# Folding the masked node groups before the scatter, gathering 3 and 4 tiles in turn, and reordering the setup of a four-layer graph kernel

## The chip, the cores and the metric

One core of one Trainium2 chip runs the whole program. The metric is device time in microseconds (us) of one launch. The chip's engines are named PE (TensorE, the matmul array), PEld (its weight loads), DVE (VectorE), ACT (ScalarE), POOL (GpSimd) and SP (SyncE, which only issues DMAs here).

## The reference, cut to what matters

Four message-passing layers on one graph of 3125 nodes and 100000 edges (`dst` is sorted, small node numbers being the most frequent; `src` is random), each followed by a residual and a layer norm over 16 features:

```python
edge_index = jnp.stack([src, dst])
x = _layernorm(x + L0(x, edge_index, edge_attr_16))               # mean of edge_attr_16 over dst
x = _layernorm(x + L1(x, edge_attr_48, edge_attr_3, ...))         # two equivariant convolutions, scattered by src
x = _layernorm(x + L2(x, edge_attr_2, edge_index, ...))           # edge network, gathers x[src], scatters by dst
x = _layernorm(x + L3(x, edge_index, W1, b1, W2, b2))             # two GCN layers
```

The last one, on which most of the change falls:

```python
def gcn_conv(h, W, b):
    hw = h @ W
    msg = hw[row] * norm[:, None]                       # row = src and the self loops
    return segment_sum(msg, col, num_segments=N) + b    # col = dst and the self loops
h = jnp.tanh(gcn_conv(x, W1, b1))
h = jnp.tanh(gcn_conv(h, W2, b2))
```

## The kernel before

Edges are padded to 98 groups (`NSUP`) of 1024; a group has T = 8 tiles of 128 edges, one edge to a partition. Nodes are padded to 25 blocks (`NB`) of 128. Since `dst` is sorted, a group touches only a few neighbouring blocks; DVE computes a table of windows (first block, last block, running offset) at the start, and every scatter by `dst` loops over the blocks of a group's window. A "window" below is one group with one block of its window. Passes run one after the other:

- **Setup** (lines 893 to 977): constants, the window tables, then from L945 on three blocks that only later passes need: the split of `src` into a fifth (`src_h`) and a rest (`src_v`, `src_n`), the same for `src` as rows on 98 partitions (`row_f`, `row_h`, `row_v`, stored by SP to the DRAM table `vtab`), and the unit edge vectors `rhat` (L969 to L977, with a square root on ACT).
- **Mean** (PE L665 to L684, DVE L994 to L1006): pairs of groups. SP's `load_pair` (L312) loads `edge_attr_16`, ACT and POOL split it into three bf16 parts (`high_part`, `rest_of`, `mid_part`, `low_part`; four pairs ahead), DVE makes one-hots of `dst`, PE scatters. Four pair buffers stand between them.
- **L1's two convolutions** (`for l in range(2)`), PE, ACT and DVE all busy. DVE's first product waits for POOL's gather from the table that SP stored (`s_tab`).
- **Edge pass** (p = 2), pairs of groups, gathering and scattering.
- **GCN passes** (p = 3, 4). POOL gathers the rows of the first GP = 3 tiles of a group by indirect DMA into `gr`, a ring of R = 4 groups. The other PT = 5 tiles are gathered by PE: DVE compares a broadcast row of `vtab` with the partition number (L1334, 5 instructions, `oht`), PE multiplies that one-hot with the table in SBUF (L824, 5 matmuls of 240 columns for a tile, into three PSUM banks of 2, 2 and 1 tiles), and DVE masks the result with the one-hot of the fifth (L1346, `mk`, 240 columns for a tile: 5 candidate fifths of 48, of which only one is not zero). PE then scatters by `dst`: a POOL-gathered tile takes one matmul of 48 columns (L836), a PE-gathered tile three of 80 columns (L840), 18 matmuls for a window. The one-hots of `dst` for it are made by ACT, window by window: 8 ACTIVATEs (L585) and one over all 8 tiles (L590), into a ring of R = 4 windows (`of_used` frees them). PE's program order is: gather of group s+1, scatter of group s. DVE's is: `tile_onehots(s+2)`, `select_rows(s+1)`. SP, per group: wait for POOL's gather of s, load the indices of s+4, wait for `oht` of s, load the `vtab` row of s+2. The end of a pass reduces 5 PSUM banks (L1405), adds, applies tanh, multiplies by the weights and builds the next table.

Of the kernel before, what the change touches and what calls it, by code (L numbers as in the profile page):

```python
# [38 lines left out]
GP = 3  # L39
PT = T - GP  # L40
# [7 lines left out]
ABANK = 512 // AW  # L48
# [14 lines left out]
def build(nc, a):  # L63
    with ExitStack() as ctx:
# [11 lines left out]
        mk = sb("mk", [P, 2, T, GW], BF16)  # L76
        mkf = mk[:, :, :, :].rearrange("p b t n -> p b (t n)").bitcast(F32)[:, :, 0:T * AW]\
# [82 lines left out]
        row_f = ht[0:NSUP, 0, :]  # L160
        row_h = ht[0:NSUP, 1, :]
# [61 lines left out]
        of_used = {p: sem(f"of_used{p}") for p in (3, 4)}  # L223
        row_used = [sem(f"row_used{p}") for p in range(2)]
# [62 lines left out]
        def _(sp):  # L287
# [20 lines left out]
            sp.wait_ge(s_rowv, 1)  # L308
            sp.dma_start(vtab, row_v).then_inc(s_vtab, 16)

            def load_pair(i, r):  # L312
                sp.wait_ge(ea_lo, i * R + r + 1)
                for b in range(2):
                    sp.dma_start(ea16[:, r, b, :, :].rearrange("p t f -> p (t f)"),
                                 e16[bass.ds(i * 2 * R + 2 * r + b, 1), :, :].rearrange("o p f -> p (o f)")).then_inc(ea_in[r], 16)

            with sp.Fori(0, PAIRS // R) as i:
                for r in range(R):
                    load_pair(i, r)  # L320
            load_pair(PAIRS // R, 0)
# [12 lines left out]
            for p in range(2):  # L334
# [8 lines left out]
                store_table(p)  # L343
                with sp.Fori(1, PAIRS) as i:
# [29 lines left out]
            def load_tail(p, b, s):  # L374
                sp.dma_start(vb[:, b, 0:PT * P], vtab[bass.ds(s, 1), GP * P:SUP].broadcast_to([P, PT * P]))\
                    .then_inc(vb_in[p][b], 16)

            for p in (3, 4):
# [3 lines left out]
                for r in range(R):  # L382
                    if p == 3 and r < 2:
                        sp.wait_ge(g_in[2][r], (QUADS + 1 - r) * 16 * T)
                    elif p == 4:
                        sp.wait_ge(g_in[3][r], (ROUNDS + (1 if r < 2 else 0)) * 16 * GP)
# [3 lines left out]
                def refill_ring(i, r, more):  # L390
                    s = i * R + r
                    if more:
                        sp.wait_ge(g_in[p][r], (i + 1) * 16 * GP)
# [17 lines left out]
        def _(pool):  # L411
# [25 lines left out]
            def gather(p, b, seen):  # L437
# [3 lines left out]
                for t in range(T if p == 2 else GP):  # L441
# [47 lines left out]
        def _(act):  # L489
# [13 lines left out]
            root(rn_root, rn[:, :, :].rearrange("p s t -> p (s t)"))  # L503
# [8 lines left out]

            high_part(0, 0, 1)
            with act.Fori(0, PAIRS // R) as i:
                for r in range(R):
                    high_part(i * R + (r + 1), (r + 1) % R, i + (1 if r + 1 < R else 2))
                    mid_part(i * R + r, r)
            mid_part(PAIRS - 1, 0)
            act.wait_ge(s_par, 16 * 21)
            node_root()  # L520
            node_root()
            for l in range(2):
# [51 lines left out]
            for p in (3, 4):  # L574
                def window_onehots(i, r):
                    s = i * R + r
                    lo, hi, off = load_window(act, s)
                    with act.Fori(lo, hi) as c:  # L578
# [4 lines left out]
                        for t in range(T):  # L583
# [3 lines left out]
                        act.wait_ge(of_abs[p], (off + c) * T + T)  # L587
                        act.sem_inc(s_turn, 1)
                        oh = oh_f[:, bass.ds(turn, 1), :, :].rearrange("p o t n -> p (o t n)")
                        nc.scalar.activation(oh, oh, ACT.Relu, bias=ones[:, 0:1], scale=-1.0).then_inc(of_ready[p], 1)  # L590

                act.sem_inc(of_abs[p], BIAS * T)
# [13 lines left out]
        def _(pe):  # L606
# [53 lines left out]
            pe.wait_ge(s_par, 16 * 21)  # L660

            for bk in range(4):
                zero_bank(bk)
            def mean_step(j, r):  # L665
# [20 lines left out]

            for l in range(2):
# [117 lines left out]
            for p in (3, 4):  # L805
                for bk in range(5):
# [5 lines left out]
                def sums_of(c):  # L812

                    at = pe.snap(c * AW + ((c * 43) >> 8) * (512 - ABANK * AW), min_val=0, max_val=5 * 512 - AW)
                    return at

                def gather_tiles(s, b):

                    pe.wait_ge(oht_done[p], s * NC + NC)
                    for g in range(3):  # L820
                        pe.wait_ge(mk_done[p], s * 3 + (g + 1))
                        for t in range(2 * g, min(2 * g + 2, PT)):
# [4 lines left out]
                        mm.then_inc(gm_done[p], 1)  # L827
# [668 lines left out]
```

## Time and profile before

| | |
|---|---|
| median of 3 runs | 4139.42 us (4136.7 to 4139.91) |
| profiled execution | 4135.05 us, of it 4133.2 us span |
| busy share of the span | PE 84%, DVE 79%, ACT 71%, POOL 65% |
| mean | about 71.5 to 246 us |
| L1, first and second convolution | 270 to 1350, 1393 to 2421 us |
| edge pass | 2445 to 3062 us |
| GCN passes 3 and 4 | 3110 to 3604, 3625 to 4118 us |
| mean granted TensorE clock | 0.93 |

Times in the profile count from the first instruction. The time of a run is about 2 us more than the span. The boundaries of the passes were read off the timeline.

### The profile page before, as it was taken

To read this page: it belongs to the slowest core of one execution; us is meant where nothing else is said; L and a number is where in the kernel's file an instruction comes from. 1 tells how busy PE (TensorE), PEld (TensorE's weight loads), DVE (VectorE), ACT (ScalarE), POOL (GpSimd) and SP (SyncE) were. 2 spreads that over 40 slices of the span, in tenths; PEclk is the share of its full clock that TensorE was granted. 3 is DMA by queue.
4 is the path that set the end of the run, shared out by engine and by line. 5 is a ranking of instruction groups with operands and counts; after the bars stand their busy time and mean duration, and the time that the engine had idled before them with its cause. 6 is when DMAs were issued, how large, how long until landed. Compare 5 with 4: busy or idle time off the path is not lost.

```text
span 4133.2 us, 104667 instructions
## 1 busy us (share of the span) xinstructions
PE 3490.8 (84%) x29279; PEld 2953.1 (71%) x29280; DVE 3285.2 (79%) x6447; ACT 2937.3 (71%) x4368; POOL 2696.7 (65%) x2653
## 2 busy tenths in 40 slices
PE   1569999999999699999999967778868988789886
PEld 1448888888888477777777757777757777678775
DVE  7769999999999688888888878888877765577655
ACT  1239999999999599999999930000017888888887
POOL 2547777777776577777777747776626655366553
PEclk9999999999999799999999988777769998899988
DMA  5112111111111311111111111111103222122221
GB/s 62 37 21 25 24 25 24 24 25 24 25 24 23 23 30 30 30 29 30 31 30 31 30 21 31 29 29 26 26 8 49 47 39 37 26 49 46 39 38 24
DMA packets 282518, 126.21 MB, mean 31 GB/s; under 512 B 178158, under 2 KB 257202, under 8 KB 282486
## 3 DMA queue, kind: packets, MB, share of 16 engines
q1 hardware_dynamic: 200950, 97.56, 10.1%
q0 software_dynamic: 81536, 28.26, 8.0%
q8 instruction: 16, 0.26, 0.0%
q14 instruction: 16, 0.13, 0.0%
HBM read 123.81 MB, written 1.78 MB: 30 GB/s over the span
## 4 chain that ended last, share of the span: by engine, by line
PE 26%; issue 21%; POOL 17%; DVE 13%; ACT 11%; ACTq 6%; DVEq 3%; DMA 2%; SPq 1%; POOLq 0%
POOL gb L452 16%; PE ps L706 10%; PE ps L722 10%; ACT rest L585 9%; ACTq L585 2%; ACTq L280 2%; PE ps L712 2%; PE ps L619 2%; DVE oht L1266 2%; DVE oh L989 2%; DVE rest L1005 1%; ACTq L578 1%; PE ps L824 1%; DVE xt L1091 1%; ACT v L571 1%
## 5 line engine op out<-in xcount | busy, mean ns | idle before, releaser
L452 POOL DMA_INDIRECT gb<-table,idx x1568 | 1617.2, 1031 | 555.0 <-issue 450.1
L442 POOL DMA_INDIRECT gb<-table,idx x980 | 984.6, 1005 | 710.3 <-issue 432.2
L706 PE MATMUL ps<-big,oh 128*128 128x290 f32 (+1 forms) x7840 | 1264.0, 308 | 1.7 <-DVE big L1131 1.7
L706 PEld LDWEIGHTS ps<-big,oh 128*128 128x128 f32 x7840 | 1069.7, 191 | 124.5 <-DVE big L1131 2.2
L722 PE MATMUL ps<-w,ht 128*128 128x320 f32 x3136 | 1007.7, 444 | 103.7 <-DVE xt L1091 102.1
L532 ACT ACTIVATE oh<-iota_f,src_n 128x640 fp32r<-128x640 f32 x1372 | 1024.5, 815 | 0.0
L535 ACT ACTIVATE oh<-oh,ones 128x2560 fp32r<-128x2560 f32 (+1 forms) x392 | 849.6, 2167 | 12.8
L722 PEld LDWEIGHTS ps<-w,ht 128*128 128x128 f32 x3136 | 556.9, 191 | 365.3 <-DVE xt L1091 173.6
L1091 DVE TENSOR_TENSOR xt<-ps,gb 128x640 f32<-128x640 f32 x784 | 643.8, 821 | 91.1 <-PE ps L722 27.2
L585 ACT ACTIVATE rest<-rest,dst_f x1952 | 595.9, 387 | 116.7 <-issue 96.1
L824 PE MATMUL ps<-tabb,oht 128*128 128x240 bf16 x4900 | 593.9, 283 | 35.6 <-DVE oht L1334 13.4
L1099 DVE TENSOR_REDUCE msg<-xt 128x80 f32<-128x1280 f32 (+1 forms) x392 | 580.7, 1482 | 0.0
L824 PEld LDWEIGHTS ps<-tabb,oht 128*128 128x128 bf16 x4900 | 495.0, 104 | 100.6 <-issue 31.4
L1346 DVE TENSOR_TENSOR mk<-ps,oh_h 128x480 bf16<-128x480 f32 (+1 forms) x588 | 316.5, 570 | 277.1 <-PE ps L824 272.8
L571 ACT ACTIVATE v<-v 128x384 fp32r<-128x384 f32 x98 | 51.3, 523 | 561.0 <-DVE v L1281 437.2
L1131 DVE TENSOR_TENSOR big<-parts,oh_h 128x1160 fp32r<-128x1160 f32 (+1 forms) x392 | 426.9, 1089 | 0.2
L775 PE MATMUL ps<-tabb,oht 128*128 128x80 bf16 x5880 | 293.6, 229 | 73.7 <-DVE mk L1295 60.7
L775 PEld LDWEIGHTS ps<-tabb,oht 128*128 128x128 bf16 x5880 | 287.1, 118 | 79.4 <-DVE mk L1295 65.5
L1334 DVE TENSOR_SCALAR oht<-eat,pid_c 128x640 bf16<-128x640 f16 x980 | 322.2, 394 | 24.8 <-DMA eat<-vtab 24.6
L590 ACT ACTIVATE rest<-rest,ones x244 | 280.1, 1148 | 30.0
L619 PE MATMUL ps<-v,oh 128*128 128x96 f32 x1168 | 178.9, 316 | 79.1 <-DVE oh L989 72.7
L525 ACT ACTIVATE ht<-ps,b 113x512 f32<-113x512 f32 x196 | 134.6, 687 | 151.4 <-PE ps L712 151.4
(225 smaller groups left out, 2672.6 us busy)
## 6 DMA issues: line engine op xcount, KB each, us to landing
gb<-table,idx POOLq DMA_INDIRECT x2548, 2.4
eat<-in_eat SPq DMA_DIRECT2D x196, 192.0 KB, 2.4
eat<-vtab SPq DMA_DIRECT2D x196, 160.0 KB
eat<-vtab SPq DMA_DIRECT2D x49, 256.0 KB
rest<-in_edge_attr SPq DMA_DIRECT2D x98, 64.0 KB, 1.8
idx<-in_src SPq DMA_DIRECT2D x245, 4.0 KB
idx<-in_dst SPq DMA_DIRECT2D x196, 4.0 KB, 1.6
ea<-in_edge_attr SPq DMA_DIRECT2D x1, 784.0 KB, 19.5
```

Source lines behind the costliest of these rows:

```text
L442: nc.gpsimd.indirect_dma_start(out=(gb if p == 2 else gr)[:, b, t, 0:tabw[p]], out_offset=None, in_=tabs[p], in_offset=bass.IndirectOffset ...
L452: nc.gpsimd.indirect_dma_start(out=gb[:, b, t, 0:tabw[p]], out_offset=None, in_=tabs[p], in_offset=bass.IndirectOffsetOnAxis(ap=idx[:, b, ...
L532: nc.scalar.activation(oh5[:, b, t, :], iota_f[:, 0:CW], ACT.Abs, bias=src_n[:, bass.ds(s, 1), t]).then_inc(a_abs[l], 1)
L535: nc.scalar.activation(oh5[:, b, t0:t1, :], oh5[:, b, t0:t1, :].bitcast(F32), ACT.Relu, bias=ones[:, 0:1], scale=-1.0).then_inc(a_done[l], 1)
L585: nc.scalar.activation(oh, iota_h[:, bass.ds(c * P, P)], ACT.Abs, bias=dst_f[:, bass.ds(s, 1), t], scale=-1.0).then_inc(of_abs[p], 1)
L706: mm = nc.tensor.matmul(out, oh5[:, b, t, c * P:(c + 1) * P], big[:, b, t, 0:W], start=False, stop=False, skip_group_check=True)
L722: mm = nc.tensor.matmul(ps[:, WPAIR[l][t // 2 % 2] + c, 0:MJ * D], ht[:, b, (t // 2) * P:(t // 2 + 1) * P], w2[l][:, c, :], start=True, st ...
L775: mm = nc.tensor.matmul(ps[:, 5 + g, u * AW:(u + 1) * AW], oht[:, k, c, e:e + P], tabk[:, c, part, :, :], start=(c + part == 0), stop=(c = ...
L824: mm = nc.tensor.matmul(ps[:, 5 + g, (t % 2) * GW:(t % 2 + 1) * GW], oht[:, b, c, t * P:(t + 1) * P], tabc[:, c, :, :], start=(c == 0), st ...
L1091: V.tensor_tensor(pv, wv, repeat(xin, 2, J_), ALU.mult).then_inc(p_done[l], 1)
L1099: V.tensor_reduce(msg[:, b, 4 * h:4 * h + 4, 0:J_], pv, AX.X, ALU.add).then_inc(r_done[l], 1)
L1131: V.tensor_tensor(big[:, b, 4 * h:4 * h + 4, 0:NH * MP[l]].rearrange("p t (h f) -> p t h f", h=NH), repeat(parts[l][:, b, 4 * h:4 * h + 4, ...
```

## The change

1. **Fold (`compact_rows`, new).** After the masks, DVE adds the five candidate fifths of every PE-gathered tile together in three bf16 adds: 96 columns to 96, 48 to 48, and the last 48 into `mc`. Only one fifth is not zero. PE scatters the folded row with one matmul of 48 columns, so a window takes 8 matmuls in place of 18. The sums fill 3 PSUM banks in place of 5, zeroed and reduced accordingly.
2. **3 and 4 tiles in turn.** Even groups keep 3 POOL-gathered tiles, odd groups get 4 (`GPS`); PE gathers 5 or 4 (`TAIL`), the latter in two PSUM banks.
3. **Setup.** The `src` split and `rhat` move on DVE from ahead of the mean to behind the table of L1's first convolution; the row split moves behind the table of the second one, and SP's store of `vtab` with it. `load_pair` moves from SP's queue to ACT's, four pairs ahead by hand. PE's wait for the parameters moves behind the mean. ACT's root of `rn` comes third, not first.

```diff
@@ PE: scatter, GCN
                 def scatter_tiles(at, ohs, r):
                     for t in range(T):
-                        if t < GP:
-                            mm = nc.tensor.matmul(psf[:, bass.ds(at, 3 * D)], ohs(t), gr[:, r, t, 0:3 * D // 2].bitcast(BF16),
-                                                  start=False, stop=False, skip_group_check=True)
-                        else:
-                            for n in range(3):
-                                mm = nc.tensor.matmul(psf[:, bass.ds(at, AW)], ohs(t), mk[:, r % 2, t - GP, n * AW:(n + 1) * AW],
-                                                      start=False, stop=False, skip_group_check=True)
+                        rows = gr[:, r, t, 0:3 * D // 2].bitcast(BF16) if t < GPS[r % 2] else mc[:, r % 2, t - GPS[r % 2], :]
+                        mm = nc.tensor.matmul(psf[:, bass.ds(at, 3 * D)], ohs(t), rows,
+                                              start=False, stop=False, skip_group_check=True)
...
-                    pe.wait_ge(mk_done[p], s * 3 + 6)
+                    pe.wait_ge(mc_done[p], s + 1)
@@ POOL
-                for t in range(T if p == 2 else GP):
+                for t in range(T if p == 2 else GPS[b % 2]):
@@ DVE: GCN
+                def compact_rows(s, b):
+                    m = TAIL[b]
+                    dve.wait_ge(mk_done[p], s * 3 + 6)
+                    V.tensor_tensor(mk[:, b, 0:m, 0:6 * D], mk[:, b, 0:m, 0:6 * D], mk[:, b, 0:m, 6 * D:12 * D],
+                                    ALU.add).then_inc(ad_done[p], 1)
+                    dve.wait_ge(ad_done[p], s * 2 + 1)
+                    V.tensor_tensor(mk[:, b, 0:m, 0:3 * D], mk[:, b, 0:m, 0:3 * D], mk[:, b, 0:m, 3 * D:6 * D],
+                                    ALU.add).then_inc(ad_done[p], 1)
+                    dve.wait_ge(ad_done[p], s * 2 + 2)
+                    V.tensor_tensor(mc[:, b, 0:m, :], mk[:, b, 0:m, 0:3 * D], mk[:, b, 0:m, 12 * D:15 * D],
+                                    ALU.add).then_inc(mc_done[p], 1)
                 def step(i, r, more):
...
                         select_rows(s + 1, 1 - r % 2)
+                        compact_rows(s + 1, 1 - r % 2)
@@ ACT: loads of the mean
+            for r in range(R - 1):
+                load_pair(0, r)
             high_part(0, 0, 1)
-            with act.Fori(0, PAIRS // R) as i:
+            with act.Fori(0, PAIRS // R - 1) as i:
                 for r in range(R):
                     high_part(i * R + (r + 1), (r + 1) % R, i + (1 if r + 1 < R else 2))
                     mid_part(i * R + r, r)
+                    if r == 0:
+                        load_pair(i, R - 1)
+                    else:
+                        load_pair(i + 1, r - 1)
```

Not shown: the DVE lines that move whole (L945 to L953 and L964 to L977 to behind L1073; L955 to L962 to behind L1211), the constants, and the semaphore counts that follow from them.

## Rows read from the trace of the kernel before

**Rows 1.** Busy time by stretch; columns PE, PEld, DVE, ACT, POOL, clock, DMA.
```profile
core 0: us, PE busy (x) PEld busy (x) DVE busy (x) ACT busy (x) POOL busy (x), PEclk, DMA share, GB/s
...
71.50:246.40 174.90, 93.80 (x1218) 82.18 (x1218) 128.90 (x220) 34.32 (x91) 86.30 (x91) 1.00 0.12 34
...
270.50:1350.00 1079.50, 1056.50 (x5678) 864.83 (x5678) 991.27 (x1568) 979.39 (x974) 825.21 (x779) 1.00 0.14 24
...
3110.00:3604.00 494.00, 421.09 (x4695) 363.87 (x4695) 324.98 (x868) 422.73 (x1063) 277.04 (x290) 0.92 0.23 41
```

**Rows 2.** Waits in pass 3: who for whom, us, times, longest.
```profile
DVE mk L1346 <- PE ps L824: 137.6, 124, 5.0
...
PE ps L836 <- ACT rest L590: 46.7, 23, 2.5
...
ACT rest L585 <- PE ps L840: 10.9, 3, 5.3
```

**Rows 3.** Timeline of ACT in pass 3, window starts; 12 windows left out.
```profile
3121.48 2.45 ACT L585 ACTIVATE rest<-rest,dst_f  x8 [5.29 <-PE ps L840]
...
3180.64 2.44 ACT L585 ACTIVATE rest<-rest,dst_f  x8 [0.48 <-issue]
3184.26 2.43 ACT L585 ACTIVATE rest<-rest,dst_f  x8
```

**Rows 4.** Timeline of one group in pass 3.
```profile
3133.44 2.73 PE L824 MATMUL ps<-tabb,oht 128*128 128x240 bf16 x25
3133.48 0.19 DVE L1328 TENSOR_TENSOR oh_h<-src_h,iota_f 128x25 f32<-128x25 f32 x1 [0.16 <-DVE mk L1346]
3133.65 1.68 DVE L1334 TENSOR_SCALAR oht<-eat,pid_c 128x640 bf16<-128x640 f16 x5
...
3134.90 0.95 POOL L442 DMA_INDIRECT gb<-table,idx  x1 [0.30 <-issue]
3135.26 1.52 DVE L1346 TENSOR_TENSOR mk<-ps,oh_h 128x480 bf16<-128x480 f32 x3
...
3136.94 0.19 DVE L1328 TENSOR_TENSOR oh_h<-src_h,iota_f 128x25 f32<-128x25 f32 x1 [0.16 <-DVE mk L1346]
```

**Rows 5.** Timeline of pass 3's last groups and end.
```profile
3587.13 4.40 PE L824 MATMUL ps<-tabb,oht 128*128 128x240 bf16 x25
...
3602.01 1.18 PE L840 MATMUL ps<-mk,rest 128*128 128x80 bf16 x15
...
3603.30 3.01 DVE L1405 TENSOR_REDUCE t<-ps 128x96 f32<-128x480 f32 x5 [7.95 <-PE ps L830]
```

**Rows 6.** Timeline of DVE in the setup.
```profile
22.45 0.53 DVE L946 CAST src_f<-src_i 128x784 f32<-128x784 int32 x1
...
37.80 0.69 DVE L956 CAST ht<-acc 98x1024 f32<-98x1024 int32 x1 [9.57 <-DMA acc<-in_src_row]
...
66.98 2.61 DVE L977 TENSOR_TENSOR rhat<-rhat,rn 128x2352 f32<-128x2352 f32 x1
...
71.55 0.23 DVE L1000 TENSOR_SCALAR rest<-dst_f,rest 128x16 f16 x1 [1.96 <-issue]
```

**Rows 7.** Timeline of DVE where L1's two convolutions begin.
```profile
257.38 0.57 DVE L1072 COPY tab<-x 128x400 f32<-128x400 f32 x1
...
270.50 0.82 DVE L1091 TENSOR_TENSOR xt<-ps,gb 128x640 f32<-128x640 f32 x1 [12.55 <-DMA gb<-table,idx]
...
1392.74 0.26 DVE L1141 TENSOR_TENSOR vprod<-gb,rhat 128x96 f32<-128x96 f32 x1 [22.43 <-DMA gb<-table,idx]
```

**Rows 8.** Groups of POOL: edge pass (first row), pass 3 (second).
```profile
L442 POOL DMA_INDIRECT gb<-table,idx x392 | 422.2, 1077 | 203.5 <-issue 151.3 <-DVE v L1281 51.3 <-DMA idx<-in_src 0.9
...
L442 POOL DMA_INDIRECT gb<-table,idx x290 | 277.4, 956 | 197.6 <-PE ps L830 111.7 <-issue 85.9
```

**Rows 9.** Groups of DVE by form: a mask of two tiles.
```profile
L1346 DVE TENSOR_TENSOR mk<-ps,oh_h 128x480 bf16<-128x480 f32 x392 | 253.9, 655 | 275.5 <-PE ps L824 271.4 <-issue 1.5
```

**Rows 10.** DVE's line 1005, duration ns min/median/max.
```profile
L1005 DVE TENSOR_TENSOR rest<-rest x146: 678/692/1165, 71.8 to 244.8; 128x1024 bf16<-128x1024 f16 x146
```

More of the change, by code:

```diff
@@ L38 @@
 EH = 64
-GP = 3
-PT = T - GP
+GPS = (3, 4)
+GP = min(GPS)
+OA = T
+TAIL = [T - n for n in GPS]
+GROUPS = [[2, 2, n - 4] for n in TAIL]
 MID = NP_ // 2
@@ L223, in build @@
         of_used = {p: sem(f"of_used{p}") for p in (3, 4)}
+        ad_done = {p: sem(f"ad_done{p}") for p in (3, 4)}
+        mc_done = {p: sem(f"mc_done{p}") for p in (3, 4)}
         row_used = [sem(f"row_used{p}") for p in range(2)]
@@ L343, in _ @@
                 store_table(p)
+                if p == 1:
+                    sp.wait_ge(s_rowv, 1)
+                    sp.dma_start(vtab, row_v).then_inc(s_vtab, 16)
                 with sp.Fori(1, PAIRS) as i:
@@ L501, in stat_root, with load_pair @@
                 root(sv_root[:, :], sv[:, 0:D])
-            root(rn_root, rn[:, :, :].rearrange("p s t -> p (s t)"))
+            def load_pair(i, r):
+                act.wait_ge(ea_lo, i * R + r + 1)
+                act.sem_inc(s_turn, 1)
+                for b in range(2):
+                    nc.scalar.dma_start(ea16[:, r, b, :, :].rearrange("p t f -> p (t f)"),
+                                        e16[bass.ds(i * 2 * R + 2 * r + b, 1), :, :].rearrange("o p f -> p (o f)")).then_inc(ea_in[r], 16)
             def high_part(j, r, seen):
@@ L517, in _ @@
                     mid_part(i * R + r, r)
+                    if r == 0:
+                        load_pair(i, R - 1)
+                    else:
+                        load_pair(i + 1, r - 1)
+            for r in range(R):
+                high_part(PAIRS - R + r, (r + 1) % R, PAIRS // R + (r + 1) // R)
+                mid_part(PAIRS - R - 1 + r, r)
+                if r == 0:
+                    load_pair(PAIRS // R - 1, R - 1)
+                elif r == 1:
+                    load_pair(PAIRS // R, 0)
             mid_part(PAIRS - 1, 0)
-            act.wait_ge(s_par, 16 * 21)
             node_root()
             node_root()
+            root(rn_root, rn[:, :, :].rearrange("p s t -> p (s t)"))
+            act.wait_ge(s_par, 16 * 21)
             for l in range(2):
@@ L582, in window_onehots @@
                         act.sem_inc(s_turn, 1)
-                        for t in range(T):
+                        for t in range(OA):
                             oh = oh_f[:, bass.ds(turn, 1), t, :].rearrange("p o n -> p (o n)")
@@ L805, in _ @@
             for p in (3, 4):
-                for bk in range(5):
+                for bk in range(-(-NB // ABANK)):
                     zero_bank(bk)
@@ L1211, in _ @@
                     dve.sem_inc(s_node, 1)
+                    dve.wait_ge(s_row, 16)
+                    link(V.tensor_copy(row_f, row_i))
+                    link(V.tensor_scalar(row_h, row_f, float(CW), None, ALU.is_ge))
+                    for k in range(2, NH):
+                        link(V.scalar_tensor_tensor(out=row_h, in0=row_f, scalar=float(k * CW), in1=row_h,
+                                                    op0=ALU.is_ge, op1=ALU.add))
+                    V.scalar_tensor_tensor(out=row_v, in0=row_h, scalar=-float(CW), in1=row_f,
+                                           op0=ALU.mult, op1=ALU.add).then_inc(s_rowv, 1)
                 else:
```

113 lines of the change are left out of this document (51 added, 62 removed).

## Prediction

> **What bounds the kernel now.** I first cut the span into its passes with the table of stretches [rows 1] and asked of each which engine has no room. The change touches three places.
>
> In the setup and the mean nothing is full: DVE is busy 128.90 of 174.90 us of the mean, and it works alone on the path before it. The timeline shows when the mean may begin: the window tables are ready at 22.45 us, but the first one-hot starts at 71.55 us, behind blocks that the mean doesn't read, one of them preceded by an idle wait of 9.57 us for a DMA [rows 6]. L1's first convolution is PE's (1056.50 of 1079.50 us), so a shift of its start moves everything behind it by as much.
>
> In passes 3 and 4 PE is busy 421.09 of 494.00 us and ACT 422.73 [rows 1], which alone names no bound. The waits do: ACT's L585 waited for PE's scatter only 3 times, 10.9 us in all, while PE waited for ACT's L590 23 times and DVE for PE 124 times [rows 2]. The rest of ACT's idle time is its own issue. ACT's windows start every 4.23 us (59.16 us for the 14 windows from 3121.48 to 3180.64), and 3.62 us apart where a second window of the same group follows, at 3184.26, for the first time in group 19 [rows 3]. So the pass goes at ACT's pace, 122 windows of about 4.05 us, and ACT's work is what the change leaves alone. The scatter's matmuls, which the change cuts from 18 to 8, are not on that path.
>
> **Setup.** DVE's work from 22.45 to 69.6 us (end of L977 [rows 6]) leaves the head of the mean: the first one-hot comes 71.55 − 24.5 = 47.0 us earlier, if the 1.96 us of loop entry stay. It can come so early only if pair 0 is loaded and split. SP used to issue these loads at 45 us, behind everything; ACT can now issue from about 15 us, when POOL's reduction has passed. Loading then takes place beside the big strided loads. I take 1.5 us for that, so −45.5 us. Bounds: 0 lost, and 13.3 lost if the new loads queue behind SP's until `src_row` has landed at 37.8 [rows 6]: 37.8 minus 24.5.
>
> ACT's six to eight extra DMA issues per four pairs cost nothing: ACT is busy 34.32 of 174.90 us in the mean [rows 1], and the four buffers of a ring hide its latency. If they didn't, each of 49 pairs would lose up to the length of two issues, under 1 us.
>
> What comes back: behind `tab` (end 257.95) DVE idled 12.55 us until the gathered rows were there [rows 7]. Now the `src` split takes 5.8 us (22.45 to the end of L953 at 28.2), the constants 2.1, and the `rhat` block 22.8 (46.8 to 69.6, its wait for ACT's root included): 30.7 us. The first product comes 30.7 − 12.5 = 18.2 us later. POOL's gathers, PE's weights and ACT's one-hots are then ready earlier than needed, but each of them has small buffers, so nothing is won by it. The row split (37.80 to 44.25, 6.4 us) goes under the 22.43 us in which DVE waits before 1392.74 [rows 7]; the store of `vtab` behind it delays SP's later loads by as much, and they are due 10 us a group. Cost nothing; without that cover 6.4 us. The 9.57 us of waiting vanish. Sum of the setup: −45.5 + 18.2 = −27.3 us (from −28.8 to −15.5).
>
> **Passes 3 and 4, what is removed.** At the end of a pass, behind ACT's last window, 15 + 3 matmuls become 8: 1.18 us of L840 [rows 5] become some 0.5, so −0.65. L1405's five reductions of 3.01 us [rows 5] become two of 480 elements and one of 240, some 1.7: −1.3. Early in the pass window 5 is released by a scatter (5.29 us of ACT's waiting [rows 3]), which is 10 matmuls shorter: −0.4. Together −2.4 us a pass. Zeroing 3 banks, not 5, is hidden under DVE's building of the table.
>
> **What is added.** DVE's round for a group takes 3.46 us when nothing keeps it waiting (3133.48 to 3136.94 [rows 4]). The three adds stand nowhere in this trace. Nearest from below are 16-bit operands in SBUF: 1024 elements in 0.692 us [rows 10], 25 elements in 0.19 [rows 4], so 0.49 ns an element beyond 0.18: 480, 240 and 240 elements take 0.42 + 0.30 + 0.30 and 0.03 us for each wait on its own result, 1.1 us. Nearest from above is the mask, 480 elements in 655 ns [rows 9]: 0.66 + 0.42 + 0.42 + 0.09 = 1.6 us. I take 1.1, since both operands are 16-bit there as here. An odd group has a fifth less of `oht` (−0.32), 240 fewer masked elements (−0.24) and adds of four fifths the size (1.0). So DVE needs 4.6 and 3.9 us in turn, 4.25 on average (4.7 with the upper price), against ACT's 4.23 in groups of one window.
>
> POOL: gathers start 1.25 us apart (0.95 and 0.30 idle [rows 4]), 3.75 us a group. Now 3.5 a group: 4.38 us. And they get company: in the edge pass, where DVE runs many instructions with both inputs in SBUF, the same gather takes 1077 ns, not 956 [rows 8], which makes 3.5 × 1.377 = 4.82 us. I take 1.30 a gather, 4.55 us: DVE's new adds are short and fill about a fifth of its round. The Trainium skill (SBUF — State Buffer, "Who interferes with whom") says that a VectorE instruction with two SBUF inputs contends with a GpSimd instruction that reads SBUF, and that the later one blocks until the other is done. The masks of before have one input in PSUM, the adds two in SBUF, so by this rule the adds speak against this change; by row alone (4.38) a pass would lose 2.7 us, by the edge pass's number 10.6 (below).
>
> So POOL at 4.55 and DVE at 4.25 are both slower than ACT's 4.23, but only where groups have one window. That is so for groups 1 to 18. From there on two-window groups give 24 windows for 20 groups up to group 39, then more, about 4.9 us a group, and ACT is the bound again. What ACT falls behind in the first stretch it never regains: (4.55 − 4.23) × 18 = 5.8 us, less a little that the ring has in hand, 5.5. Bounds: (4.38 − 4.23) × 18 = 2.7, or 0 if the ring takes it, and (4.82 − 4.23) × 18 = 10.6.
>
> The PE queue loses 10 matmuls a window and 2.5 a group; PE was waiting for ACT anyway. Nobody waits longer behind DVE's adds: PE reads the folded row only after the gather of the next group, 2.73 us at full clock [rows 4].
>
> A pass: −2.4 + 5.5 = +3.1, both +6.2.
>
> **Sum.** −27.3 + 6.2 = −21.1 us. From the profiled 4135.05 us that gives 4114.0; the median of the runs is 4.4 us higher, so 4118.3, say 4118.
>
> **Rivals.**
> *Passes 3 and 4 stay ACT's in full.* For: DVE idles 137.6 us a pass, POOL's average is under ACT's 5.04 a group. Against: both averages hide the first stretch. −28 − 4.8 gives 4106.
> *POOL is blocked as in the edge pass.* For: the rule above and 1077 ns. Against: the adds are shorter than the edge pass's 1.2 us one-hots. 10.6 to 12 a pass: −27.3 − 4.8 + 24 = −8, 4131.
> *The new loads come late.* For: in 15 to 33 us SP's loads fill the DMA engines. Against: separate queues. The mean begins 13.3 us later: 4118 + 12 = 4130. The Trainium skill (DMA: Bandwidth & Descriptors, "Issuing engines are not separate DMA queues") says that DMAs started by different engines run on the same 16 engines and interleave; by this the loads would be neither free nor last in line.
> *TensorE's clock falls, on the other side.* PE has less to do, and its clock in pass 3 was already 0.92 of full [rows 1]; where it waited for ACT it fell to 1.2 GHz and 25 gather matmuls took 4.40 us, not 2.73 [rows 4, 5]. At that level a one-window group costs 22.5 matmuls × 0.176 = 4.0, the scatter 0.7 and about 0.6 of gaps, 5.3 us against ACT's 4.23. Over the first 39 groups, 43 windows and 171 us, that is up to 34 us a pass: −27.3 − 4.8 + 68 = +36, 4175. It decides where more than half of those groups run at the low clock. Against: at 5.3 us PE would have no pauses, and in the stretches where it had none the clock was up.
>
> **Chances.** Forecast 0.50 (its own range 4110 to 4126), ACT's pace kept 0.17, POOL blocked 0.12, late loads 0.13, clock 0.05, something else 0.03. A measurement here tells 0.2%, 8.3 us, from no change, so below 4131.1 is faster. The first two are, with half of the next two: 0.78. The other halves are "same", with part of the rest: 0.16. Slower 0.06. The range: 4105 to 4135 takes in the kept pace, blocked POOL and late loads, and leaves out the clock and the case in which two of the bad ones meet.
>
> **What would show it.** The first L1000 at 24 to 27 us; the last matmul of the mean near 200; the first L1091 near 243; from there to pass 3 everything 27 us earlier and otherwise alike. In passes 3 and 4: three adds of 0.42, 0.30 and 0.30 us; L442 between 0.97 and 1.02 us; ACT waiting for PE's scatter in the first 20 groups, some 0.3 us a window on average, and hardly after; passes of 495 to 500 us. Wrong would be: L1000 after 35 us; ACT waiting in the second half of a pass; a mean clock under 0.8 there; adds over 0.5 us.

## The result, and the profile after

| | before | changed |
|---|---|---|
| median of 18 runs, us | 4137.81 (4134.86 to 4142.38) | 4130.03 (4124.27 to 4134.66) |
| ratio, 95% interval | 1 | 0.9981 (0.9973 to 0.9988) |
| span of the profiled execution, us | 4133.2 | 4131.1 |

The change gained 7.8 us, 0.19%; from the same median the forecast of 4118 us is a gain of 19.8. The measured 4130.03 us lies inside the stated range of 4105 to 4135, but the gain is less than half of the 21.1 us that the sum gave. One thing must be known to read the experiments: they were timed in five sets, each with runs of the kernel before beside them, and that kernel took 4,141 us in the second set and 5,101 to 5,104 us in the other four, so ratios are compared within a set alone. Of stretches, the mean can be compared across sets: from its first window to its last, five kernels with the setup of before took 172.33 to 172.43 us, in whichever set they ran.

The spans of the two profiled executions differ by 2.1 us, the medians by 7.8. A term that is read from one trace late in the kernel is therefore good to some 6 us only; the mean's terms are much better than that.

The table of stretches, changed kernel: the mean, L1's first convolution, pass 3 (columns as in [rows 1]).

```profile
24.70:216.70 192.00, 94.39 (x1221) 82.12 (x1219) 136.44 (x220) 38.55 (x100) 86.73 (x98) 1.00 0.23 46
259.20:1340.50 1081.30, 1057.87 (x5679) 865.71 (x5679) 991.28 (x1570) 979.28 (x974) 815.81 (x768) 0.99 0.14 24
3101.00:3599.00 498.00, 404.61 (x3235) 321.19 (x3235) 383.50 (x1108) 422.95 (x1063) 321.86 (x339) 0.85 0.24 38
```

The timeline of DVE, changed kernel: the mean's first one-hot, the first step behind the mean, the first product of L1 and of its second convolution, the sums at the end of pass 3.

```profile
24.75 0.23 DVE L979 TENSOR_SCALAR rest<-dst_f,rest 128x16 f16 x1 [2.22 <-issue]
...
216.64 0.18 DVE L1040 TENSOR_SCALAR r<-ps 128x25 f32<-128x25 f32 x1 [0.86 <-PE ps L698]
...
259.26 0.82 DVE L1096 TENSOR_TENSOR xt<-ps,gb 128x640 f32<-128x640 f32 x1
...
1382.77 0.26 DVE L1146 TENSOR_TENSOR vprod<-gb,rhat 128x96 f32<-128x96 f32 x1 [15.86 <-DMA gb<-table,idx]
...
3599.06 1.79 DVE L1436 TENSOR_REDUCE t<-ps 128x160 f32<-128x480 f32 x3 [7.53 <-PE ps L847]
```

Against [rows 6, 7, 5] the first one-hot is 46.8 us earlier (line 979 prepares it, so its start is taken as the mean's). L1's first product is only 11.2 us earlier, its second convolution 10.0, the end of pass 3 4.2, the end of the span 2.1. The mean, 174.90 us before [rows 1], takes 192.00. The loss is there.

Where in the mean? DVE's line 979 (1000 before) runs once for each of the 73 windows. From the first start to the last it is 172.40 us before (71.55 to 243.95) and 189.46 after (24.75 to 214.21). The first 8 of these 72 spacings take 19.52 and 24.84 us, the other 64 take 152.88 and 164.62. So 17.06 us are two losses: 5.32 at the start and 11.74 spread over all the rest. The timeline at the start, changed kernel:

```profile
23.65 1.28 ACT L509 ACT_TABLE_LOAD   x1 [23.49 <-PEq L674]
...
24.95 0.72 ACT L509 ACTIVATE rest<-rest 128x256 bf16<-128x256 f32 x2
...
25.45 1.85 POOL L418 TENSOR_TENSOR rest<-rest 128x256 f32<-128x256 f32 x2 [10.61 <-ACT rest L509]
...
28.48 1.17 PE L688 MATMUL ps<-rest 128*128 128x49 bf16 x16 [2.85 <-POOL rest L423]
...
29.28 1.68 DVE L984 TENSOR_TENSOR rest<-rest 128x1024 bf16<-128x1024 f16 x2 [1.32 <-PE ps L688]
...
32.45 0.42 ACT L509 ACTIVATE rest<-rest 128x256 bf16<-128x256 f32 x1 [3.67 <-DMA rest<-in_edge_attr]
```

ACT may split the first pair only when PE has released its buffer (L674), which PE does behind its wait for the setup. DVE begins the one-hots of pair 0 at 25.02 us, but the product waits for the split until 28.48, 3.73 us after line 979 first starts. Before, four pairs had been split long ahead, and the same distance was 1.10 us (71.55 to 72.65). The last line shows the second part of the price: ACT then waits 3.67 us for a load of a later pair.

The groups of DVE over the last 65 windows, kernel before (first fence) and changed kernel (second): first the one-hots themselves (two for a window), then the step ahead of them. Idle time stands behind the second bar.

```profile
L1005 DVE TENSOR_TENSOR rest<-rest 128x1024 bf16<-128x1024 f16 x128 | 97.9, 806 | 4.2 <-PE ps L674 2.0
L1000 DVE TENSOR_SCALAR rest<-dst_f,rest 128x16 f16 x65 | 15.8, 243 | 36.1 <-DVE rest L1005 32.8 <-issue 3.3
```

```profile
L984 DVE TENSOR_TENSOR rest<-rest 128x1024 bf16<-128x1024 f16 x128 | 103.1, 846 | 3.8 <-PE ps L688 1.7
L979 DVE TENSOR_SCALAR rest<-dst_f,rest 128x16 f16 x65 | 16.2, 249 | 42.2 <-issue 23.5 <-DVE rest L984 18.7
```

The loss has two halves at the same code. The idle time ahead of the window's first step rose by 6.1 us (36.1 to 42.2), and the label changed with it: "issue", time that nothing in the profile releases, went from 3.3 us to 23.5. The one-hots got slower by 5.2 us (97.9 to 103.1). One of them takes 0.69 us, or some 0.47 us more; of the 130 of these windows 35 were long before and 45 are now. The changed kernel's timeline has both kinds:

```profile
65.25 1.29 DVE L984 TENSOR_TENSOR rest<-rest 128x1024 bf16<-128x1024 f16 x2
...
66.00 1.08 POOL L418 TENSOR_TENSOR rest<-rest 128x256 f32<-128x256 f32 x1 [0.85 <-ACT rest L509]
...
67.66 0.23 DVE L979 TENSOR_SCALAR rest<-dst_f,rest 128x16 f16 x1 [1.11 <-issue]
...
67.88 0.66 POOL L418 TENSOR_TENSOR rest<-rest 128x256 f32<-128x256 f32 x1 [0.17 <-ACT rest L509]
67.93 2.23 DVE L984 TENSOR_TENSOR rest<-rest 128x1024 bf16<-128x1024 f16 x2
...
68.50 1.12 POOL L423 TENSOR_TENSOR rest<-rest 128x256 bf16<-128x256 f32 x1
```

Two one-hots take 1.29 us, and 2.23 us where POOL's subtractions run beside both. Such windows are 2 of 65 before, with 1.7 us of POOL's work beside them, and 12 of 65 now, again with 1.7. So a later turn also moves DVE's one-hots onto POOL's subtractions. That this overlap is what lengthens them is read from the timelines; no run took it away by itself.

A pair with one window mostly takes 2.43 or 2.37 us before and 2.67 after. The 64 spacings hold 40 turns of the outer loop, which took 101.5 us before and 110.25 after, 0.22 us more each. The 24 second windows of a pair, which the inner loop brings, took 51.4 and 54.4 us; 12 of them before and 11 now come after the shortest time, 1.89 or 1.90 us. So it is the turn of the outer loop that got slower, and the longer one-hots add to it.

### The profile page after: what moved, and what is told of

Read it like the earlier page. It is cut to its first block, busy times and chain, and to the rows that moved or that the text cites. A ratio compares the mean times of both kernels' runs of the same rounds, so it can differ in the third digit from the quotient of the medians.

```text
span 4131.1 us, 99865 instructions
## 1 busy us (share of the span) xinstructions
PE 3454.0 (84%) x26345; PEld 2866.4 (69%) x26346; DVE 3410.5 (83%) x6933; ACT 2938.7 (71%) x4369; POOL 2786.3 (67%) x2751
## 4 chain that ended last, share of the span: by engine, by line
PE 25%; issue 22%; POOL 18%; DVE 14%; ACT 10%; ACTq 6%; DVEq 4%; DMA 2%; POOLq 0%; SPq 0%
POOL gb L448 16%; PE ps L721 10%; PE ps L737 10%; ACT rest L601 8%; ACTq L601 2%; PE ps L727 2%; DVE oht L1280 2%; ACTq L286 2%; DVE oh L968 1%; POOL gb L438 1%; PE ps L635 1%; DVE rest L984 1%; ACTq L594 1%; DVE xt L1096 1%; ACT v L587 1%
## 5 line engine op out<-in xcount | busy, mean ns | idle before, releaser
L448 POOL DMA_INDIRECT gb<-table,idx x1568 | 1620.5, 1033 | 571.4 <-issue 451.4
L438 POOL DMA_INDIRECT gb<-table,idx x1078 | 1075.1, 997 | 630.2 <-issue 452.6
L841 PEld LDWEIGHTS ps<-tabb,oht 128*128 128x128 bf16 x4410 | 469.6, 110 | 121.3 <-DVE mk L1363 31.5
L1363 DVE TENSOR_TENSOR mk<-ps,oh_h 128x480 bf16<-128x480 f32 (+1 forms) x490 | 273.9, 596 | 160.4 <-PE ps L841 159.9
L790 PEld LDWEIGHTS ps<-tabb,oht 128*128 128x128 bf16 x5880 | 294.1, 120 | 84.5 <-DVE mk L1309 70.6
L1349 DVE TENSOR_SCALAR oht<-eat,pid_c 128x640 bf16<-128x640 f16 (+1 forms) x980 | 313.2, 385 | 30.8 <-DMA eat<-vtab 29.3
```

Source lines behind the costliest of these rows:

```text
L438: nc.gpsimd.indirect_dma_start(out=(gb if p == 2 else gr)[:, b, t, 0:tabw[p]], out_offset=None, in_=tabs[p], in_offset=bass.IndirectOffset ...
L448: nc.gpsimd.indirect_dma_start(out=gb[:, b, t, 0:tabw[p]], out_offset=None, in_=tabs[p], in_offset=bass.IndirectOffsetOnAxis(ap=idx[:, b, ...
L790: mm = nc.tensor.matmul(ps[:, 5 + g, u * AW:(u + 1) * AW], oht[:, k, c, e:e + P], tabk[:, c, part, :, :], start=(c + part == 0), stop=(c = ...
L841: mm = nc.tensor.matmul(ps[:, 5 + g, (t % 2) * GW:(t % 2 + 1) * GW], oht[:, b, c, t * P:(t + 1) * P], tabc[:, c, :, :], start=(c == 0), st ...
```

## Experiments

**Which part costs what.** The setup part alone, and the convolution part alone, each on the kernel before (the hunks of the diff, nothing new).

> The setup part alone (row splits, unit directions and constants behind the mean, the loads of edge_attr_16 issued by ACT), with the graph convolutions of before. Theory 1 (the two parts are independent, and each has the price seen in the trace of the changed kernel): the first product of L1 stands at 259 us in place of 270.5, the mean needs 192 us from its first to its last window in place of 175, passes 3 and 4 keep their lengths, and the time is 9 to 11 us under before (ratio 0.9974 +- 0.0004). Rival (part of the loss in passes 3 and 4 came from the setup's shift, through the throttle of TensorE's clock): passes 3 and 4 are longer here as well, by 2 us or more together, and the time is only 5 to 8 us under before.

> The convolution part alone (fold of the masked groups, one scatter matmul for each tile, POOL 3 and 4 tiles in turn), with the setup of before. Theory 1: the mean and L1 stand where they stand before (first product of L1 at 270.5 us), and passes 3 and 4 together cost 6.8 us more, so the time is 4144 to 4146 us (ratio 1.0016 +- 0.0004). Rival (the loss in the passes is an interaction with the setup part): the ratio is 1.0005 or less.

Both were timed in the first set, with the kernel before at 5,104 us. The setup part gave 0.9939 (0.9913 to 0.9964); its 72 spacings took 188.09 us (24.76 to 212.85), so the mean's loss belongs to the setup part. The convolution part gave 1.0248 (1.0218 to 1.0278), far from either expectation. It was run again:

> The same kernel as b_conv: the convolution part alone. Theory: passes 3 and 4 cost 6.8 us together and nothing else moves, so the ratio to before is 1.0016 +- 0.0005. Rival (they cost this only together with the setup part): 1.0005 or less.

In the second set: 1.0011 (1.0002 to 1.0020), 3.5 us slower by the medians, with 6.8 just inside the interval's 0.8 to 8.3 us. The parts are independent as far as this can tell. What the other sets show is taken up at the end.

**The mean: is it the loads?** First the loads of `edge_attr_16` back on SP, ACT's loop as before; then SP's other loads held back.

> The changed kernel with the loads of edge_attr_16 issued by SP again, behind its 25 setup loads; everything else as changed. Theory T1 (the loads in ACT's queue are what makes each pair of the mean slower): one pair with one window takes 2.43 us again, and from its first to its last window the mean needs about 175 us plus what its start costs. Theory T2 (where DVE's loop lies among its instructions, once the setup steps ahead of it are gone, makes each turn of the outer loop some 0.2 us longer): a pair still takes 2.67 us, and the drift of 12 us over 49 pairs stays. Either way the first pairs wait longer for their rows, since they are issued behind SP's other loads: the first window at 30 to 45 us in place of 24.75. By T1 the mean ends near 210 to 220 us, by T2 near 222 to 235 us.

> The changed kernel with all of SP's loads behind dst held until eight pairs of the mean have been split (one wait on POOL's low parts): src, edge_attr_3, edge_attr_2, x, the row form of src and the parameters, none of which is used before the mean ends at 217 us. Theory (the first 5.3 us that the mean lost by window 8 came from its rows landing beside these big loads): the gap to the spacing of before by window 8 falls from 5.3 us to 1 us or less, the later drift of 0.24 us per pair stays unless it too is made by the loads, and the mean ends at 211 to 214 us; time 3 to 5 us under the changed kernel. Rival (the early loss is ACT's issue time or the order of the steps, not the big loads): the mean ends at 216 to 218 us as in the changed kernel, and the time is equal to it. If T1 holds, holding the loads has no effect on the later drift.

```diff
             sp.dma_start(dst_i[:, :, :], dstv).then_inc(s_dst, 16)
+            sp.wait_ge(ea_lo, R + 8)
             sp.dma_start(src_i[:, :, :], srcv).then_inc(s_src, 16)
```

With SP's loads the last 64 spacings took 165.28 us, so T1 falls: who issues the loads has nothing to do with the drift. (The first window came at 24.82 us all the same, not at 30 to 45, and the mean ended at 236.9.) What ACT's issuing does buy is the start; with SP DVE waited 23.40 us for the second pair, behind SP's own loads:

```profile
51.02 2.18 DVE L976 TENSOR_TENSOR rest<-rest 128x1024 bf16<-128x1024 f16 x2 [23.40 <-PE ps L680]
```

With the other loads held back the first 8 spacings took 23.43 us in place of 24.84, the rest 163.37. So the loads beside SP's big ones cost 1.4 us, near the 1.5 that the prediction took for it, and not the 5.3 that this experiment's theory gave it; 3.9 us of the early loss stay. The 1.4 is a difference of two traces from different sets, and the first 8 spacings of kernels with this code range from 24.84 to 25.39 us.

**The mean: is it the loop's place?** Semaphore increments that nobody waits for, ahead of the window tables, move the loop along DVE's stream. Places are counted in the built program: the outer loop's 21 instructions begin at the 65th in the changed kernel and at the 92nd before.

```diff
+            for _ in range(27):
+                dve.sem_inc(s_idle, 1)
             dve.wait_ge(s_extp, 1)
```

> The changed kernel with 27 semaphore increments, which nothing waits for, put into DVE's stream ahead of the window tables, so that the mean's loop stands at the place among DVE's instructions (the 92nd to the 112th) that it had before; nothing else is changed. Theory T2 (the place of the loop makes each turn 0.24 us longer): a pair with one window takes 2.43 us again, the last window starts 12 us sooner after the first than in the changed kernel (about 177 us in place of 189.5), the mean ends at 204 to 206 us, and the time is 10 to 12 us under the changed kernel's. Rival (the turns are longer for something that the streams of the other engines, or the data in flight, bring): a pair takes 2.67 us, and the mean ends at 216 to 218 us.

> The changed kernel with one semaphore increment ahead of DVE's window tables: the mean's loop begins at DVE's 66th instruction in place of the 65th, counted in the built program. If what counts is the place by a small step (the loop's head at a multiple of 2, 4 or more), a pair with one window takes 2.43 us at once; if it is how far from the start of the stream the loop lies, or a boundary that the longer shift of 27 crossed, it stays 2.67 us.

> The changed kernel with one more semaphore allocated and nothing that uses it, so the semaphores named behind it have other numbers and no instruction moves. If the one extra instruction of k_pad1 was what ended the drift (the loop's place), a pair with one window takes 2.67 us here as in the changed kernel; if it was the semaphores' numbers, 2.43 us.

> The kernel before with five semaphore increments ahead of DVE's window tables: the mean's loop begins at DVE's 97th instruction, 32 behind its place in the changed kernel, so with the same remainder by 4, 8, 16 and 32. If the remainder counts, a pair with one window takes 2.67 us in place of 2.43, and the mean is 11 to 12 us longer with nothing else changed; if the distance from the start counts, it stays 2.43 us.

> The kernel before with 37 semaphore increments ahead of DVE's window tables: the mean's loop begins at DVE's 129th instruction of the built program, 64 behind its place in the changed kernel (the 65th). If the loop is slow where its head comes at a multiple of 64 instructions, a pair with one window takes 2.67 us and the mean 11 to 12 us more, in a kernel whose work is otherwise that of before; if it stays at 2.43 us, a period of 64 is out as well, and what the place means stays open.

> The changed kernel with three short steps (the identity, the node numbers and the mask of real nodes) moved from ahead of the mean behind it, so that the mean's loop begins at DVE's 62nd instruction of the built program in place of the 65th, and all its setup stays otherwise as changed. If there is a boundary in the stream between the 65th and the 66th instruction, with the loop's head ahead of it and its body behind, a turn of the outer loop still crosses it here, and a pair with one window takes 2.67 us; if only that one place of the head is slow, 2.43 us, and the time is 11 us under the changed kernel's.

> The changed kernel with 256 semaphore increments ahead of DVE's window tables: the loop begins at DVE's 321st instruction, 256 behind its place in the changed kernel. 
| kernel | loop begins at | last 64 spacings, us |
|---|---|---|
| before | 92nd | 152.88 |
| before + 5 | 97th | 152.83 |
| before + 37 | 129th | 152.93 |
| changed | 65th | 164.62 |
| changed, one semaphore more, no instruction | 65th | 164.35 |
| changed + 1 | 66th | 153.55 |
| changed + 27 | 92nd | 154.02 |
| changed, three steps moved away | 62nd | 162.11 |
| changed + 256 | 321st | 163.00 |

Each row is one trace; other kernels with the head at the 65th and nothing added (setup part, 3 gathers, 4 gathers, no adds) give 163.0 to 164.9 us, so the two levels lie some 10 us apart with a spread of 2.

The group of line 979's counterpart in the changed kernel + 27 (with its one-hots), + 1 and + 256, one fence for each:

```profile
L987 DVE TENSOR_TENSOR rest<-rest 128x1024 bf16<-128x1024 f16 x128 | 98.5, 810 | 4.2 <-PE ps L689 2.2
L982 DVE TENSOR_SCALAR rest<-dst_f,rest 128x16 f16 x65 | 15.7, 241 | 36.3 <-DVE rest L987 31.9 <-issue 4.4
```

```profile
L982 DVE TENSOR_SCALAR rest<-dst_f,rest 128x16 f16 x65 | 15.8, 243 | 35.8 <-DVE rest L987 31.5 <-issue 4.3
```

```profile
L982 DVE TENSOR_SCALAR rest<-dst_f,rest 128x16 f16 x65 | 16.2, 249 | 42.8 <-issue 22.5 <-DVE rest L987 20.2
```

One instruction more takes "issue" from 23.5 us to 4.3, and the idle time from 42.2 to 35.8; with 27 more the one-hots are back at 98.5 us, 36 of 130 long. So both halves of the loss hang on the loop's place. With the head at the 66th, all of the loop lies behind the place between the 65th and the 66th; with the head at the 65th or 62nd the loop crosses it twice in a turn. The idle time that this adds is 6.1 us over 40 turns, 0.15 us a turn; with what it does to the one-hots a turn takes 0.22 us more. With the head 256 instructions further on the same happens; at 92, 97 and 129 it doesn't. The first boundary is pinned to one place, between the 65th and the 66th. The second lies somewhere in the loop's 21 instructions from the 321st on, so 256 to 275 behind the first. The fast places exclude one each 32 or each 64 (the 97th and the 129th lie 32 and 64 behind the 65th); one each 128 was not tried. (The 256 increments took 22.4 us, the first window coming at 47.14, more than the 5 to 16 expected.)

The changed kernel + 27 was timed in the second set and gave 0.9938 (0.9923 to 0.9953), 4116.32 us: the change as written with its loop elsewhere is 24.3 us faster than before. The mean gives 10.9 us of what it has over the changed kernel. Between L1's first product (248.33) and the first product of the second convolution (1367.04; 259.26 and 1382.77 in the changed kernel) another 4.8 us come, which were not expected. The increments move every later loop of DVE too. By the built programs the loop of L1's first convolution, 77 instructions and 48 turns, begins at the 172nd in the changed kernel, at the 179th before and at the 199th with the 27. The traces of the second set and of the result fall apart the same way:

| kernel | L1's loop begins at | first product to that of the second convolution, us |
|---|---|---|
| before | 179th | 1122.24 |
| convolution part alone | 179th | 1123.62 |
| changed | 172nd | 1123.51 |
| changed, 3 gathers | 172nd | 1125.77 |
| changed + 27 | 199th | 1118.71 |
| faults of the mean mended (below, also with the 27) | 199th | 1117.21 |

DVE's idle time put down to "issue" ahead of line 1096 falls from 24.9 to 20.2 us with the 27. A boundary 128 behind the first, between the 193rd and the 194th, would do this, some 0.1 us a turn; one each 256 would not touch this loop in any of the six. No mean loop of the first table lies across the 193rd. So 128 fits both tables, but no run moved L1's loop by itself, and the distance stays open.

**What the passes pay.** The fold kept with 3 gathers in each group; the fold's adds left out; 4 gathers in each group.

```diff
-GPS = (3, 4)
+GPS = (3, 3)
```

> The changed kernel with POOL gathering 3 tiles of every group, as before, and the fold kept, so DVE masks 5 tiles of every group. Theory (POOL's 3.5 gathers a group are what lost 0.2 us in each of the 18 groups with one window): ACT sets these groups' pace again, the 3.7 us that each pass lost by its 24th window go, and the time is 5 to 8 us under the changed kernel's. Rival (DVE, with the masks and adds of a group, is as late as POOL): the groups take 4.5 us or more, each pass loses 1 to 3 us more than in the changed kernel, and the time is 2 to 6 us over the changed kernel's.

> The changed kernel with the three adds of the fold left out: the scatter reads the first 48 of the 240 masked columns (so four of the five node groups are left out of the masked tiles' rows), in one matmul for a tile as before. Theory (DVE's masks and adds, 4.3 us a group where POOL's gathers and TensorE's products allow it, set the pace of the 18 groups with one window): DVE has 0.9 us a group less to do, ACT sets the pace again, the first 24 windows of a pass take 107 to 110.5 us in place of 114.3 and 111.2, and the time is 5 to 8 us under the changed kernel's. Rival (POOL's four gathers in every second group): the first 24 windows keep 111 to 114 us, and the time is within 2 us of the changed kernel's.

> The changed kernel with POOL gathering 4 tiles of every group, so DVE masks and adds 4. Theory (DVE sets the pace): DVE has 0.5 us a group less than with 3.5 gathered tiles' average, but POOL then needs 4 gathers of 0.95 us and the gaps between them, near 4.3 to 5 us a group; if POOL becomes the bound, the first 24 windows of a pass take 114 to 120 us, and the time is 2 to 15 us over the changed kernel's. Rival (POOL can keep 4 gathers a group inside 4.3 us): ACT sets the pace and the time is 3 to 6 us under the changed kernel's.

The windows of a pass are marked by the start of ACT's Relu. Pass 4 first. From the 9th to the 17th there is one window a group: 33.68 us before (4.21 a group), 34.55 in the changed kernel (4.32), 34.61 in the convolution part alone (4.33), 34.92 with 3 gathers (4.37). In pass 3 the same eight groups take 33.88, 35.02, 34.18 and 34.21 us, and in the changed kernel + 27, the same code, 33.98 and 34.22 in the two passes. So the eight groups tell before (4.21 to 4.24 a group) from the fold (4.25 to 4.38), but not the variants of the fold from each other. The table of stretches for these eight groups in pass 4, changed kernel, then 3 gathers and fold:

```profile
3649.27:3683.82 34.55, 29.12 (x239) 23.42 (x239) 30.96 (x91) 28.75 (x72) 26.27 (x28) 0.92 0.26 45
```

```profile
3651.62:3686.54 34.92, 31.93 (x276) 25.84 (x273) 33.60 (x97) 28.88 (x72) 24.90 (x25) 1.00 0.26 48
```

And POOL's group in the same stretch of the changed kernel:

```profile
L438 POOL DMA_INDIRECT gb<-table,idx x28 | 26.6, 951 | 8.5 <-issue 8.5
```

In the changed kernel POOL waits for nothing but its own issue: 26.6 + 8.5 us fill the 34.55, so POOL has no room. With 3 gathers POOL has room and DVE is busy 33.60 of 34.92 us, so DVE is the likely bound. The first 24 windows take 112.1 and 110.4 us in passes 3 and 4, against 110.3 and 107.1 before and 114.3 and 111.2 changed: part of the loss comes back, not all, and both theories are half right. The time was 0.9972 (0.9962 to 0.9982) of before, 4129.32 us, not to be told from the changed kernel's.

The other two were timed in two of the other sets, with the kernel before at 5,104 and at 5,101 us:

> The same kernel as i_noadds (the fold's adds left out). From the trace of the changed kernel, POOL issues a gather each 1.25 us without a break in the groups with one window, 4.37 us for a group of 3.5, and ACT needs 4.21. Theory (POOL sets this pace, DVE does not): groups 8 to 16 still take 4.33 to 4.4 us, and the first 24 windows 111 to 114 us. Rival (DVE's adds set it): 4.2 us, and 107 to 110.5 us.

> The same kernel as l_44 (4 gathers in every group). Theory (POOL's 1.25 us a gather sets the pace): groups with one window take 5.0 us, so the first 24 windows of a pass take 14 us more than with 3.5, two passes 25 to 30 us, and the time is 4150 to 4165 us. Rival (POOL has slack that the trace does not show): 4125 to 4132 us.

Without the adds 1.0189 and 1.0180, with 4 gathers 1.0442 and 1.0431, all four outside what was expected, which was reckoned from the second set's times. From the first to the 25th window, passes 3 and 4 took there: 134.9 and 131.1 us with 3 gathers and no fold (the setup part alone), 149.8 and 145.5 with 3.5 and the fold, 149.1 and 146.2 with 3.5 and no adds, 164.1 and 162.5 with 4. That is some 15 us for each half gather a group (the first of them together with the fold), and nothing for the adds. For the condition of the second set these runs don't settle whether the adds go unnoticed with 3.5 gathers; POOL's row above says so, no run does.

**The two faults of the mean mended, convolutions left alone.**

> The setup part with the graph convolutions of before, with SP's loads behind dst held until eight pairs are split, and with the 27 increments ahead of the window tables. If T2 holds and the parts add: first window at 25 us, last at 198 to 200 us, first product of L1 at 244 us, and the time 26 to 28 us under before (ratio 0.9935). If T2 falls: the last window at 211 to 213 us, and 12 to 14 us under before (ratio 0.9968).

In the second set: 4112.42 us, 0.9930 (0.9916 to 0.9943), the lowest of all, 28.2 us under before; its interval overlaps that of the changed kernel + 27. First window 24.79, last 202.65, first product 247.7. It stays 3 us behind what was expected of the mean, mostly because its first product waits for the split of pair 0 as described above: the first 8 spacings still take 23.19 us, against 19.52. Letting PE release ACT's buffers ahead of its wait for the setup is the next thing to do; it wasn't tried.

## Why the prediction was wrong

- **The mean starts 47.0 us earlier:** 46.8. Right.
- **"I take 1.5 us for that":** the step that failed. It stood for the whole price of starting the mean early, and that price was 17.1 us. Its named cause, loads beside SP's big ones, did measure 1.4 us. What was missing: 11.7 us because taking 27 instructions away put the loop's head at the 65th instruction (27 instructions put back, and one alone, took 10.6 and 11.1 us of it away; about half of it is idle time of the turn, the other half one-hots slowed beside POOL's subtractions), 2.6 us because the splits no longer ran ahead (3.73 less 1.10 us, read from the timeline, not tried), and some 1.3 us that stay unassigned, 0.5 of them the loop's place within the first 8 spacings. The extra issues on ACT, taken at nothing, cost nothing in the drift.
- **30.7 us behind the table, 12.5 under the idle time, 18.2 net:** from the end of the mean to the first product it was 24.12 us before and is 42.62 now, 18.5 more. Right. The row split is covered: DVE still waits 15.86 us before the second convolution, against 22.43 [rows 7].
- **Setup −27.3:** −11.2. The whole error sits in the step above. With the loop moved, L1's first product came 22.2 us earlier than before.
- **+3.1 us a pass:** from the start of pass 3 to the end of the span 7.1 us of the shift were lost in the traces, where 6.2 were forecast; the convolution part alone cost 3.5 us (0.8 to 8.3) by the medians. Right within that, and in the stretch that was named, though the terms differ. A group with one window went from 4.21 or 4.24 us to 4.25 to 4.38, not to 4.55, and the first eight windows of a pass take part of the loss. The first 24 windows, the start of the pass among them, cost 4.0 and 4.1 us more (110.3 to 114.3, 107.1 to 111.2). The reductions gained 1.2 us (3.01 to 1.79), the adds took 0.41, 0.29 and 0.29 us in the larger size, forecast at 0.42, 0.30 and 0.30.
- **A gather between 0.97 and 1.02 us:** 0.951 beside the adds, 0.956 before [rows 8]. The prediction weighed a rule of the Trainium skill (SBUF — State Buffer, "Who interferes with whom"), by which a VectorE instruction with two SBUF inputs contends with a GpSimd instruction that reads SBUF. For the gathers this trace shows no such thing. In the mean, where DVE's one-hots and POOL's subtractions both have two inputs in SBUF, the long instructions (1.16 us in place of 0.69, 1.12 in place of 0.66) agree with it.
- **The clock:** 0.85 in pass 3 after 0.92, so it fell, and not under the 0.8 that was named. What it cost, if anything, no run isolates.

The rival "the new loads come late" came near the measured time, at 4130, by another mechanism than the one that acted. Two slips in the sums change nothing: with ACT's pace kept, −27.3 and −4.8 give 4107, not 4106, and the listed chances of "faster" add up to 0.80, not 0.78.

## What to carry to other kernels

When code is moved out from ahead of a short loop, the loop's place in its engine's stream moves too. If its engine's idle time goes up with "issue" as its cause, at unchanged code, put one idle instruction ahead of it before looking further: here that took the idle time away and the slower one-hots with it. Compare the busy time of the loop's instructions too, and the whole idle time, not the part under one label alone: "issue" rose by 20.2 us, the idle time by 6.1 and the busy time by 5.2. When an idle stretch is cut out of a setup, ask which other engines used it to run ahead: their lead is part of its price.

## What the runs showed of the hardware that was not expected

A boundary in DVE's instruction stream between the 65th and 66th instruction, and another 256 to 275 on, adds 0.15 us of idle time to a loop turn that crosses it both ways (42.2 against 36.1 us over 40 turns), and 0.22 us with the one-hots that here come to lie beside POOL's work. The page of the changed kernel counts the instruction queue's transfers:

```profile
q8 instruction: 15, 0.25, 0.0%
```

0.25 MB in 15 packets are 16.7 KB each. The Trainium skill (Advanced Engine Details and Errata, "ISA Cache") gives lines of 16 KB, 256 instructions, and two of them. A distance of 256 agrees with the mean's loops, but the times of L1's loop speak for one of 128, and no run decides. The price of a crossing is not on that page, and the packets are too few for a reload in each of 49 turns.

In the four sets in which the kernel before took 5,101 to 5,104 us the engines went slower while POOL gathered. The timeline of TensorE and of POOL, setup part alone, in pass 4:

```profile
4563.47 0.18 PE L838 MATMUL ps<-zeros 128*128 128x32 bf16 x1 [0.69 <-issue]
4564.88 0.26 PE L832 MATMUL ps<-tabb,oht 128*128 128x240 bf16 x1 [1.24 <-issue]
4566.30 0.26 PE L832 MATMUL ps<-tabb,oht 128*128 128x240 bf16 x1 [1.16 <-issue]
```

```profile
4562.29 0.94 POOL L431 DMA_INDIRECT gb<-table,idx  x1 [0.30 <-issue]
4563.54 0.94 POOL L431 DMA_INDIRECT gb<-table,idx  x1 [0.30 <-issue]
4564.79 0.94 POOL L431 DMA_INDIRECT gb<-table,idx  x1 [0.30 <-issue]
```

PE, with nothing that the profile shows to wait for, issued one matmul each 1.4 us beside gathers 1.25 us apart. Half a gather a group is 12 gathers in 24 groups, 15 us at 1.25 us each, which fits the 15 us above, and makes the convolution part 2.5% slower where it costs 0.1% otherwise. What differed in these sets stays open. The changed kernel itself was not timed there; its variants that keep both parts (loads on SP, loads held, three steps moved) took 1.0197 to 1.0239 of before.
